# A graph network on one core: every record scatter waits for the landing of the one before it

## The reference, cut to what matters

```python
    edge_index = jnp.stack([src, dst])
    h = jnp.maximum(_layernorm(x, axis=-1), 0.0)
    x = x + _L0_gnn_ref(h, edge_attr_3, src, dst, L0_gnn_W1, L0_gnn_b1, L0_gnn_W2)
    h = jnp.maximum(_layernorm(x, axis=-1), 0.0)
    x = x + _L1_gnn_ref(h, edge_index, edge_type_8, L1_gnn_weight, L1_gnn_bias)
    h = jnp.maximum(_layernorm(x, axis=-1), 0.0)
    x = x + _L2_gnn_ref(h, edge_index, L2_gnn_W, L2_gnn_att_src, L2_gnn_att_dst, L2_gnn_bias, L2_gnn_gamma, L2_gnn_beta)
    h = jnp.maximum(_layernorm(x, axis=-1), 0.0)
    x = x + _L3_gnn_ref(h, edge_index, L3_gnn_W, L3_gnn_b)
```

## Time and profile before

| | us |
|---|---|
| median of 3 runs | 5306.26 |
| lowest and highest | 5303.0, 5307.47 |
| span of the profiled execution | 6597.1 |
| mean granted TensorE clock in it | 0.714 of full speed |
| POOL busy in it | 3799.2 (58%) |
| of this, 784 record scatters (L577) | 766.5 |
| PE busy, DVE busy | 3895.4, 2562.6 |

### The profile page before, as it was taken

How to read it: one execution, slowest core, us unless ns; L and a number is a source line. 1 busy time by engine, 2 the same in 40 slices (tenths; PEclk the granted TensorE clock), 3 DMA queues, 4 the chain that set the end, 5 groups by cost and what they waited for, 6 DMA issues and landing times. The chain is left out here.

```text
span 6597.1 us, 65618 instructions
## 1 busy us (share of the span) xinstructions
PE 3895.4 (59%) x14913; PEld 2594.0 (39%) x14914; DVE 2562.6 (39%) x8644; ACT 1792.3 (27%) x5648; POOL 3799.2 (58%) x3942
## 2 busy tenths in 40 slices
PE   4232666667641533596455555566777777577777
PEld 2121333333320510242333333355566555455555
DVE  4223444444430300132222222255555555644443
ACT  0111555555530400011000000044444444400000
POOL 3554666666666077402666666666666666277776
PEclk7565666766665765796676666667777777688888
DMA  1011332332310010144433333323333333233332
GB/s 48 20 41 60 88 88 87 89 89 87 88 45 3 0 42 22 59 148 141 124 99 98 98 98 98 96 82 87 87 87 86 87 86 89 77 98 99 99 98 87
DMA packets 277662, 527.83 MB, mean 80 GB/s; under 512 B 80566, under 2 KB 175259, under 8 KB 277049
## 3 DMA queue, kind: packets, MB, share of 16 engines
q0 software_dynamic: 176144, 422.24, 22.5%
q1 hardware_dynamic: 85200, 86.14, 3.9%
q10 hardware_dynamic: 15960, 15.41, 0.7%
HBM read 433.63 MB, written 89.82 MB: 79 GB/s over the span
## 5 line engine op out<-in xcount | busy, mean ns | idle before, releaser
L675 POOL DMA_INDIRECT got_attend_src_dst<-dram_gtab,gather_src x832 | 800.4, 962 | 531.0 <-DVE msg_attend_src_dst L747 320.9
L577 POOL DMA_INDIRECT dram_rec_src<-rec_src x784 | 766.5, 978 | 509.6 <-issue 243.5
L1760 POOL DMA_INDIRECT got_edge_mlp_src_dst<-dram_ptab,gather_src x832 | 786.3, 945 | 463.2 <-DVE pre_edge_mlp_src_dst L1802 252.9
L1591 POOL DMA_INDIRECT got_rgcn<-dram_xtab,gather_of_type x831 | 788.3, 949 | 392.5 <-issue 187.9
L1886 PE MATMUL psS_edge_mlp_src_dst<-msg_edge_mlp_src_dst,hot_edge_mlp_src_dst 128*128 128x256 f32 x1664 | 736.1, 568 | 434.0 <-DVE sage_sums L1783 223.6
L1591 POOL DMA_INDIRECT got_gcn<-dram_htab,gather_rest x586 | 616.5, 1052 | 234.1 <-issue 148.9
L861 PE MATMUL psS_attend_src_dst<-msg_attend_src_dst,hot_attend_src_dst 128*128 128x264 f32 x1664 | 700.8, 513 | 19.5 <-DVE msg_attend_src_dst L747 14.3
L2091 PE MATMUL psO_tab<-w_tab,hT_tab 128*128 128x512 f32 (+1 forms) x980 | 474.4, 633 | 350.1 <-issue 200.5
L1886 PEld LDWEIGHTS psS_edge_mlp_src_dst<-msg_edge_mlp_src_dst,hot_edge_mlp_src_dst 128*128 128x128 f32 x1664 | 388.5, 269 | 589.7 <-issue 338.8
L1682 PE MATMUL psS_rgcn<-got_rgcn,hot_rgcn 128*128 128x257 f32 x1662 | 543.8, 471 | 79.7 <-DMA got_rgcn<-dram_xtab,gather_of_type 55.0
L1783 DVE TENSOR_TENSOR sage_sums<-sage_sums,psS_edge_mlp_src_dst 128x256 f32 x832 | 347.8, 418 | 523.6 <-PE psS_edge_mlp_src_dst L1886 246.1
(11 more groups left out here) (397 smaller groups left out, 5878.7 us busy)
## 6 DMA issues: line engine op xcount, KB each, us to landing
dram_xtab<-out_tab SPq DMA_DIRECT2D x48, 1024.0 KB
got_edge_mlp_src_dst<-dram_ptab,gather_src POOLq DMA_INDIRECT x832
got_attend_src_dst<-dram_gtab,gather_src POOLq DMA_INDIRECT x832
got_rgcn<-dram_xtab,gather_of_type POOLq DMA_INDIRECT x831
dram_rec_src<-rec_src POOLq DMA_INDIRECT x784
got_gcn<-dram_htab,gather_rest POOLq DMA_INDIRECT x586
dram_gtab<-sums ACTq DMA_DIRECT2D x48, 132.0 KB
x_sb<-x_in SPq DMA_DIRECT2D x1, 6144.0 KB
```

What stands on the lines that cost most here:

```text
L577: nc.gpsimd.indirect_dma_start(edges.to, bass.IndirectOffsetOnAxis(edges.rec[:, column, PLACE:PLACE + 1].bitcast(I32), 0), edges.rec[:, co ...
L675: nc.gpsimd.indirect_dma_start(got[:, t % U, 0:w], None, table, bass.IndirectOffsetOnAxis(row_of[:, t:t + 1], 0)).then_inc(row_in[t % U], 16)
L1591: nc.gpsimd.indirect_dma_start(got[:, t % U, 0:D], None, table, bass.IndirectOffsetOnAxis(row_of[:, t:t + 1], 0)).then_inc(row_in[t % U], 16)
L1760: nc.gpsimd.indirect_dma_start(got[:, t % U, 0:width], None, table, bass.IndirectOffsetOnAxis(row_of[:, t:t + 1], 0)).then_inc(row_in[t % ...
```

## The change

`Scatter.run` has one semaphore, `left`, in place of two. Before each scatter but the first of a stage POOL waits until all earlier scatters of the stage have landed, so that one is in flight in place of up to sixteen. The increments of `gate.step()` inside the loop are gone. The scatters, their columns, their stages and the final wait stay.

```diff
         if end > first:
-            self.left = [nc.alloc_semaphore(f"left{h}_{edges.kind}_from{first}") for h in range(2)]
+            self.left = nc.alloc_semaphore(f"left_{edges.kind}_from{first}")
 
     def run(self, pool):
         if self.end <= self.first:
             return
-        nc, edges, half = self.nc, self.edges, U // 2
-        rounds = self.end - self.first
-        for i in range(rounds):
-            for h in range(2):
-                if i:
-                    pool.wait_ge(self.left[h], 16 * half * i)
-                    self.gate.step()
-                for k in range(half):
-                    column = U * (self.first + i) + half * h + k
-                    nc.gpsimd.indirect_dma_start(
-                        edges.to, bass.IndirectOffsetOnAxis(edges.rec[:, column, PLACE:PLACE + 1].bitcast(I32), 0),
-                        edges.rec[:, column, :], None).then_inc(self.left[h], 16)
-        for h in range(2):
-            pool.wait_ge(self.left[h], 16 * half * rounds)
+        nc, edges = self.nc, self.edges
+        columns = range(U * self.first, U * self.end)
+        for n, column in enumerate(columns):
+            if n:
+                pool.wait_ge(self.left, 16 * n)
+            nc.gpsimd.indirect_dma_start(
+                edges.to, bass.IndirectOffsetOnAxis(edges.rec[:, column, PLACE:PLACE + 1].bitcast(I32), 0),
+                edges.rec[:, column, :], None).then_inc(self.left, 16)
+        pool.wait_ge(self.left, 16 * len(columns))
```

## The result

| | before | after |
|---|---|---|
| median, us | 5306.86 (4 runs, 5303.0 to 5308.14) | 6304.21 (4 runs, 6301.3 to 6308.03) |
| ratio | | 1.188, 95% interval 1.186 to 1.189 |
| span of the profiled execution, us | 6597.1, and 5303.3 in a second one (below) | 6300.4 |

The change costs 997 us, 19%. The forecast was 6110, in a range of 5860 to 6350: the right side and the right mechanism, with a price that was 194 us too small.

The account below looks back on a forecast made before the run. POOL's scatters were taken to about end five of seven scatter stages, the other two within 10 us. 5306 + 795 for the seven stages + 8 for the edge pass = 6109, said as 6110, range 5860 to 6350.

Parts of the forecast that it names:

- account of the profile's stretch: Seven scatter stages without the edge pass: 1683.5 us in the profile, taken as 1037 without a profile, ceiling 1127.
- Rival 1: Profiled stage lengths are real, so long stages hide their longer scatter chains: +156, 5462, chance 0.07.
- Rival 2: Faster: DVE starvation goes with scatters in flight, so stages fall to their chains: -316, 4991, chance 0.02.
- What ends a stage: In five of seven stages POOL's scatters about end it, in the other two within 10 us; growth to 1832, +795.
- edge pass: Its 16 scatters stand behind the last gather, hidden by the last 16 tiles in the profile: +8, 0 to 12.
- distance p: From one scatter's start to the next on POOL with the added wait: 2.33 us, against 1.263 before.
- first term: Part of p from a scatter's start to the end of its packets: 1.72 us.
- other two: Parts of p: 0.34 us for news of the landing, 0.27 until a waiting indirect DMA starts on POOL.
- Rivals 3 and 4: Cheap wait, p near 2.12: 5946, chance 0.10; dear wait, p = 2.63: 6341, chance 0.10.
- rival 4: Dear wait: p = 2.63, idle 0.30 on top or slower landings under the tables' stores: 6341, chance 0.10.
- The step: What gets nothing: SP's 1 MB stores; slower landings in table 1 might add 32 us, inside the range.
- signs to look for: In the profile after: scatter distance 2.3 us, idle about 1.4, table 1 about 750 long, span 6750, gap some 650.

Follow-up runs that it names:

- second profile of before: The kernel before run once more with no edit, for another profile: 5309.43 us, ratio 1.0002, span 5303.3.
- doubled stores: The changed kernel with each 1 MB store of the second table stage issued again into a tensor nobody reads: 6395.99 us, ratio 1.2042.

## Why the prediction was right, and what was too small

**The account of the profile's stretch** was right, against rows that showed otherwise: 1037 inferred for the seven stages, 1073.0 measured. Only the reason given for the stretch was wrong: it doesn't come with every profile of this kernel, since the second one has none. Rival 1, which took the profiled lengths as real, falls (5462, and its stage lengths with it). Rival 2 falls too: starved copies were not there to be freed. (Three sums of the working are off by 0.1: 4691.4 is 4691.3, 407.1 is 407.0, 747.5 is 747.4. Nothing rests on that.)

**What ends a stage** was more often POOL than the forecast had it, in all eight and not in five of seven. From the stage's start to its first scatter, and from its last scatter to its end, each stage takes the same in both kernels, within 0.7 us. So nothing of the longer chains is hidden anywhere. The chains, from the start of a stage's first scatter to that of its last (POOL's timeline, second profile of before and profile of the changed kernel), and what the forecast had each stage grow by:

| stage | chain before | chain after | growth | forecast |
|---|---|---|---|---|
| place | 59.9 | 113.3 | 53.4 | 50.1 |
| stats | 39.2 | 72.8 | 33.7 | 31.3 |
| table 0 | 79.6 | 151.5 | 71.9 | 67.2 |
| list by dst | 150.7 | 280.6 | 129.9 | 118.4 |
| tile | 40.1 | 73.2 | 33.1 | 24.9 |
| node update | 204.1 | 380.3 | 176.3 | 162.8 |
| table 1 | 407.5 | 886.9 | 479.4 | 340.4 |
| edge pass | 19.0 | 35.3 | 16.3 | 8 |
| sum | 1000.0 | 1993.9 | 993.9 | 803 |

**The distance p** was 2.33, put together from 1.72 + 0.34 + 0.27. Measured are 235.0 / 100 = 2.35 us in the list stage behind its loads, and 2.38 in the second table stage:

```profile
439.40:487.00 47.60, 18.58 (x13) 0.68 0.36 119
487.00:722.00 235.00, 95.55 (x100) 0.50 0.02 2
```

The first term can be read in the changed kernel's trace: in the 40 slices from 2403.21 to 2405.60 the scatter's packets are in slices 25 to 28, counted from 0, and so through 1.73 us behind its start.

```profile
GB/s 0 0 0 0 0 0 0 0 0 0 0 0 0 0 0 0 0 0 0 0 0 0 0 0 0 21 22 22 4 0 0 0 0 0 0 0 0 0 0 0
```

The other two are measured only as a sum, 0.66 there for 0.61. That the last one, POOL's start after a release, belongs in it is shown by the distance itself, which without it would be 2.06. Rivals 3 and 4 (2.12 and 2.63) fall as prices of an undisturbed landing. But rival 4 had a second reason, slower landings under the tables' stores, and this one came true in the second table stage. The mean distance of the seven stages is 1958.6 / 761 = 2.57, and its 6341 is nearer to the measured 6304 than the forecast's 6110 is. That the range held the result is owed to this bound, and not to the forecast's own term.

The Trainium skill's about 2.0 us for such a DMA ("DMA: Bandwidth & Descriptors", section "Anatomy of one DMA — SWDGE (gpsimd) path") agrees with the 2.06 of the first two terms, and has no part for POOL's start: by it the time came out at 5861, 443 too low.

**What was mis-sized** is above all the landing beside other transfers. The step said "Landings among those stores may be slower than 1.72; if half of table 1's were 0.2 late, it would be 32 us", and left it out of the sum. By the table the missing 191 us are:

| term | missing |
|---|---|
| table 1 (of it 124 beside the table work, 886.9 - 762.8) | 139 |
| list by dst | 11.5 |
| stats, tile and node update, taken as 45, 60 and 212 before, longer than their scatters' 43.3, 51.9 and 205.1 | 17 |
| distances of 2.35 to 2.41 for 2.33 in place, stats, table 0 and node update | 15 |
| edge pass | 8 |

The other 3 of the 194 are the gather stages' 5, less some 2 in the starts and ends of stages.

The list stage's 13 scatters beside its loads are 3.66 us apart, 17 us in all over 2.35. But this stage's chain was already 10.5 us over 1.263 each in the kernel before, so not all of it is new; and that the loads do it is argued from the table stage and wasn't tried by itself.

The tail of a stage, from its last scatter's start to its end, was put at 3.1 us. It is 5.3 to 11.9, in both kernels, so it cancels; of the seven stages' 36 us over the inferred 1037 it is a part. In the second table stage of the kernel before it is 10.9 us, with an end at 2220.4:

```profile
2209.46 0.96 POOL L577 DMA_INDIRECT dram_rec_src<-rec_src  x1 [0.30 <-issue]
```

**The edge pass and the gather stages.** The first was right in kind (+8, measured 15.9), but over its bound of 12, which took the scatters for hidden behind the last tiles. Undisturbed, they already end this stage in the kernel before. The last scatter, in the kernel before (stage's end 1589.1) and in the changed one (1926.0):

```profile
1581.11 0.96 POOL L577 DMA_INDIRECT dram_rec_src<-rec_src  x1 [0.30 <-issue]
...
1918.06 0.96 POOL L573 DMA_INDIRECT dram_rec_src<-rec_src  x1 [1.40 <-DMA dram_rec_src<-rec_src]
```

It is 8 us ahead of the end in both, so all of the chain's growth shows. "A gather stage that changed its length by over 10 us would be something that I have no term for": they changed by 0.2, 3.4 and 1.8 us.

**The signs to look for.** The span after was forecast at 6750, with a gap to the median of 650; it was 6300.4, with no gap. That step followed from a stretch which was taken to come with every profile. The distance (2.35 and 2.38) and the idle time of 1.43 us, ended by the scatter's own landing, came as forecast; the second table stage's last scatter came 888 us after its start, for 745.

## What to carry to other kernels

A wait for the landing of each small DMA costs the whole way from start to landing to next start, and in full where the issuing engine ends the stage, as in all eight here (that a stage with another end would hide it is argued; none here has one). Read who ends each stage before pricing it, and if the span of the profile is far from the measured time, take another profile before trusting any idle time. Two in flight hide an undisturbed latency, but beside large transfers on the same DMA engines a small one waits for them; the depth has to cover that wait, and here four did but for 9 us. Where a wait must stand, it belongs on the instruction that it guards and not on a helper ahead of it.

## What the runs showed of the hardware

- A record scatter in flight that meets a 1 MB store of SP on the DMA engines waits for it: in the distance looked at, none of its 32 packets went while 976 of the store's 1040 did. Mostly 4.7 to 5.1 us from start to start in place of 2.38; among doubled stores 4.87 us on the mean of all, for 3.47.
- With two scatters in flight and no large transfer beside them the distance is 1.26 us, as with sixteen.
- An indirect DMA on POOL that carries its wait starts so that the distance is 2.35 us; with an increment between wait and DMA it is 2.87; with the same increment ahead of the wait the time is that without it.
- One profiled execution of a kernel that runs in 5307 us had a span of 6597 us, with DVE 10.5 us idle between copies of 0.69 us. A second had none of it. What did this stays open; the runs don't tell.
